# Eight-head attention layers: scores and projections as products of 32 stationary columns, one per column tile

## The reference

```python
h = group_norm(x) * gn_w + gn_b
qkv = einsum('oc,bct->bot', qkv_w, h) + qkv_b          # 8 heads of 16 channels
w = softmax(einsum('bct,bcs->bts', q * scale, k * scale))
a = einsum('bts,bcs->bct', w, v)
out = x + einsum('oc,bct->bot', proj_w, a) + proj_b
```

## Time and profile before

| | us |
|---|---|
| median of 3 runs | 2267.47 |
| the profiled execution: time | 2267.78 |
| the profiled execution: span, first to last instruction | 2265.9 |
| PE busy | 2194.3 |
| DVE busy | 1814.8 |
| ACT busy | 1719.2 |
| POOL busy | 520.5 |

### The profile page before, as it was taken

The page is one execution under the profiler, slowest core; times in us unless marked ns, Lnnn a source line. Parts: engine busy times, 40 slices in busy tenths (PEclk is TensorE's granted clock), DMA queues, the critical chain, the costliest instruction groups (busy, mean ns, idle before and its releaser), DMA issues. The chain is left out here.

```text
span 2265.9 us, 34021 instructions
## 1 busy us (share of the span) xinstructions
PE 2194.3 (97%) x11776; PEld 972.9 (43%) x11776; DVE 1814.8 (80%) x3176; ACT 1719.2 (76%) x3107; POOL 520.5 (23%) x689
## 2 busy tenths in 40 slices
PE   2999999999999999999999999999989999999998
PEld 1233232323333232333323233333327888888887
DVE  2888888888888888888888888888837777777776
ACT  1477777777877777787777777777778888888887
POOL 3113030312203030211303031130013333333331
PEclk9999999999999999999999999999999999999999
DMA  6053343516243351625334251633111112111111
GB/s 81 4 77 54 59 62 57 82 45 91 46 66 54 58 79 48 92 42 75 54 59 70 57 78 45 86 52 62 26 45 58 59 44 67 53 48 60 41 53 49
DMA packets 81646, 132.29 MB, mean 58 GB/s; under 512 B 17632, under 2 KB 50528, under 8 KB 81504
## 3 DMA queue, kind: packets, MB, share of 16 engines
q1 hardware_dynamic: 78240, 129.70, 31.9%
q10 hardware_dynamic: 3264, 0.79, 0.2%
HBM read 53.12 MB, written 17.83 MB: 31 GB/s over the span
## 5 line engine op out<-in xcount | busy, mean ns | idle before, releaser
L449 DVE TENSOR_REDUCE h_half_nmax<-h_s_ps 128x1 f32<-128x512 f32 x2048 | 1284.7, 683 | 242.5 <-PE h_s_ps L684 233.7
L600 ACT ACTIVATE h_probs<-h_st_ps 128x512 f32<-128x512 f32 x2048 | 1103.3, 599 | 359.9 <-PE h_st_ps L821 353.7
L684 PE MATMUL h_s_ps<-h_krep,h_qrep 96*128 96x512 bf16 x2048 | 794.4, 388 | 23.8 <-SPq L234 21.9
L821 PE MATMUL h_st_ps<-h_qrep,h_krep 99*128 99x512 bf16 x2048 | 778.0, 382 | 10.9 <-ACT h_probs L600 9.9
L676 PE MATMUL h_pv<-h_probs,h_vT 128*32 128x512 f32 x4096 | 546.4, 605 | 0.9 <-ACT h_probs L600 0.7
L684 PEld LDWEIGHTS h_s_ps<-h_krep,h_qrep 96*128 96x128 bf16 x2048 | 199.8, 98 | 683.4 <-DVE h_half_nmax L449 504.8
L821 PEld LDWEIGHTS h_st_ps<-h_qrep,h_krep 99*128 99x128 bf16 x2048 | 201.5, 99 | 196.5 <-issue 35.8
L1336 PE MATMUL o_s<-o_k,o_q 128*128 128x512 f32 x768 | 223.8, 427 | 8.1 <-DVE o_q L1157 5.8
L349 POOL TENSOR_SCALAR h_nparts<-h_nmax 128x16 bf16<-128x16 f32 x64 | 16.4, 256 | 927.8 <-DVE h_nmax L457 927.8
L1336 PE MATMUL o_pv<-o_pT,o_vT 128*128 128x512 f32 x768 | 207.3, 406 | 0.8 <-ACTq L1263 0.8
L1151 DVE TENSOR_TENSOR o_pT<-o_t,o_pT 128x512 fp32r<-128x512 f32 x256 | 164.5, 684 | 44.6 <-ACT o_pT L1288 42.3
(11 more groups left out here) (116 smaller groups left out, 1379.1 us busy)
## 6 DMA issues: line engine op xcount, KB each, us to landing
h_krep<-h_kp SPq DMA_DIRECT2D x96, 256.0 KB, 8.7
h_qrep<-h_qp SPq DMA_DIRECT2D x192, 128.0 KB, 6.5
x_res<-out_dram SPq DMA_DIRECT2D x24, 512.0 KB, 3.8
num<-av SPq DMA_DIRECT2D x128, 64.0 KB
rrep<-rden_dram SPq DMA_DIRECT2D x16, 512.0 KB
out_dram<-o_y SPq DMA_DIRECT2D x16, 512.0 KB
out_dram<-h_y SPq DMA_DIRECT2D x15, 512.0 KB, 2.6
o_x_in<-out_dram SPq DMA_DIRECT2D x15, 512.0 KB, 3.5
```

The costliest lines, as they stand in the source:

```text
L449: reduce = nc.vector.tensor_reduce(half_nmax[:, c, unit:unit + 1], s_ps[bank(2 * n + c)][:, :], AX.X, ALU.max, negate=True)
L600: nc.scalar.activation(probs[g % 2][:, j, :], st_ps[bank(n)][:, :], ACT.Exp, scale=1.0 / CH ** 0.5).then_inc(exp_done, 1)
L684: nc.tensor.matmul(s_ps[bank(n)][:, :], qrep[par][0:KS, th, head, tile * P:(tile + 1) * P], krep[par][0:KS, head, c * HALF:(c + 1) * HALF] ...
L821: nc.tensor.matmul(st_ps[bank(n)][:, :], krep[par][0:KM, head, st * P:(st + 1) * P], qrep[par][0:KM, th, head, :], start=True, stop=True). ...
```

## The change

The new function `in_columns` writes one product with 128 stationary columns as four, each with 32 of the columns and into 32 partitions of the same bank. The row scores, the transposed scores and all four kinds of projection go through it; only the last of the four raises the semaphore, and only the first waits. The average and the transposes are written as before.

```diff
             def project(c, column, ready):
-                nc.tensor.matmul(misc[:, :], wg[:, column:column + P], h[:, c * HALF:(c + 1) * HALF],
-                                 start=True, stop=True).then_inc(ready, 1)
+                in_columns(misc, wg[:, column:column + P], h[:, c * HALF:(c + 1) * HALF]).then_inc(ready, 1)
...
-                    product = nc.tensor.matmul(misc[:, n * P:(n + 1) * P], h[:, t * P:(t + 1) * P],
-                                               weights, start=True, stop=True)
+                    product = in_columns(misc[:, n * P:(n + 1) * P], h[:, t * P:(t + 1) * P], weights)
...
             def project_output(c):
-                nc.tensor.matmul(misc[:, :], wo[:, 0:P], attn[:, c * HALF:(c + 1) * HALF],
-                                 start=True, stop=True).then_inc(misc_for_dve, 1)
+                in_columns(misc, wo[:, 0:P], attn[:, c * HALF:(c + 1) * HALF]).then_inc(misc_for_dve, 1)
...
+            def in_columns(to, stationary, moving):
+
+                for j in range(P // 32):
+                    columns = slice(32 * j, 32 * j + 32)
+                    product = nc.tensor.matmul(to[columns, :], stationary[:, columns], moving, start=True, stop=True)
+                return product
+
             def row_scores(n, par, quad, unit, c):
...
-                nc.tensor.matmul(s_ps[bank(n)][:, :], qrep[par][0:KS, th, head, tile * P:(tile + 1) * P],
-                                 krep[par][0:KS, head, c * HALF:(c + 1) * HALF],
-                                 start=True, stop=True).then_inc(scores_ready, 1)
+                in_columns(s_ps[bank(n)], qrep[par][0:KS, th, head, tile * P:(tile + 1) * P],
+                           krep[par][0:KS, head, c * HALF:(c + 1) * HALF]).then_inc(scores_ready, 1)
...
-                            nc.tensor.matmul(st_ps[bank(n)][:, :], krep[par][0:KM, head, st * P:(st + 1) * P],
-                                             qrep[par][0:KM, th, head, :],
-                                             start=True, stop=True).then_inc(st_ready, 1)
+                            in_columns(st_ps[bank(n)], krep[par][0:KM, head, st * P:(st + 1) * P],
+                                       qrep[par][0:KM, th, head, :]).then_inc(st_ready, 1)
```

## The result

The changed kernel takes 2276.72 us (median of 10 runs, 2272.42 to 2280.63), the kernel before 2267.43 beside it (10 runs): the ratio is 1.0039, interval 1.003 to 1.0048. It is 9 us slower; 2195 was forecast, and the time lies above the range. The profiled execution took 2280.48 us with a span of 2278.5.

What follows compares the result with a forecast made beforehand. PE was taken as the bound, busy 397.7 of 400 us. Width changes save 123 us, less 3, 21, 14 and 13, leaving 72: 2267.5 - 72 = 2195 us. The range was 2165 to 2270.

Steps and rivals of the forecast that it cites:

- the width change: Around each group's value products, switching 128 to 32 columns and back costs PE 0.24 us; removing it saves 123 us.
- an exposed weight load: Rival: every score product pays 0.025 us for weights not loaded ahead; about 2250 us, chance 0.13.
- a beat of 0.06 between starts: Rival: matmuls start no faster than a fixed beat; at 0.061 us the gain is gone, near 2267, chance 0.04.
- tiles that take turns: Rival: four tiles share reads of the moving data; at half speed a score takes 0.44 us, total 3035, chance 0.09.
- The two rules of the Trainium skill: Column tiling gives up fast weight load (estimate 2257 us); about 62 ns per microcode-decoded matmul would leave no gain.
- average: Still 128 columns wide, now between 32-column neighbours, it gets a gap taken as 0.2 us, 16 images: +3 us.
- first score waits for Q copies: At the next image's first score PE waits 1.4 us for query copies that come no earlier, 15 images: +21 us.
- statistics on DVE: The next image's statistics add 0.68 us of DVE work to each of two groups, 15 images: +14 us.
- smaller DVE and ACT places: Coefficients after the average, joining half maxima, two normalising passes: 0 to 1.8 us per image, middle taken, +13 us.
- PE waits for its instructions: Rival: more loads and matmuls per group; waiting 1.4 us for each of 135 instruction packets gives 2384 us, chance 0.09.
- gaps that come every third group: Sign in the changed profile's PE groups that PE waits for instruction packets, estimated to last 3.8 groups each.
- no gap recurs today: Evidence given against PE waiting for instructions: PE's groups in the kernel before show no recurring gap.

Runs made afterwards that it cites:

- e8: Changed kernel with the projections put back to 128 columns, only the scores in four tiles; executed once more for its profile: 2218.97 us.
- e5: Changed kernel with at most two key copies under way at a time, using two semaphores in turn: 2183.27 us, ratio 0.963.
- e6: Changed kernel with at most two key copies under way, query copies released at k = 5 and sent in pairs, at most two pairs under way: 2165.6 us, ratio 0.9552.
- e7: Changed kernel with the query copies released at k = 5 in place of k = 13 and no copies paced: 2275.91 us, one execution.
- e1: Changed kernel with SP waiting for each of the six key copies before it sends the next: 2281.05 us, ratio 1.0061.

## Why the prediction was wrong

**What bounds, and the width change: right.** The gap around the value products came from changing the column width. It went away in every plain group (2.61), and e8 put one of 0.30 at the projections. 512 x 0.24 = 123 us was right.

**The rivals on the matmul itself fell.** Four tiles take 0.39 to 0.43 us where one matmul took 0.38, and the next score follows after 0.22, four matmuls and four loads: neither an exposed weight load (a step of 0.24), nor a beat of 0.06 between starts, nor tiles that take turns. (A beat of 0.061 would have cost 8 x 0.026 = 0.21 us a group, most of the 0.24 and not all of it.) The two rules of the Trainium skill weighed in the prediction (TensorEngine Tiling, Gotcha 2; TensorE: Matmul & The Clock Gate, on 62 ns per matmul) do not set the time here.

**The smaller terms: right in kind, most of them too large.** e5, which is after without the gap, can be laid beside the sum (us):

| term | forecast | measured | from |
|---|---|---|---|
| width changes | -123 | -123 | plain group 2.85 to 2.61 |
| average | +3 | +5 | its group 3.04 - 2.61, before 2.98 - 2.85: 0.30 x 16 |
| first score waits for Q copies | +21 | +18 | e5 - e6 |
| statistics on DVE | +14 | +8 | two groups of 2.87 and 2.98, before 2.90 and 2.93: 0.50 x 15 |
| smaller DVE and ACT places | +13 | +8 | the rest |
| sum | -72 | -84 | e5 against before, 2183.27 - 2267.05 |
| PE without instructions | 0 | +93 | after - e5, 2276.72 - 2183.27 |

That the two ends nearly cancel, so that the time comes out 0.4% from before, is chance.

**The step that failed** is the dismissal of "PE waits for its instructions", which put it at nothing in the sum; measured, it cost 93 us. The prediction had named the mechanism and given it 0.09, with three faults in the working. First, it took the 1.4 us that a packet needs to move as the whole of a wait, and expected a short wait at every packet, as its sign "gaps that come every third group" says. What came was one wait in each of 15 images, 3.9 us of standing still and 2.6 of half clock; the late packet came when the key copies, 13 us of them, were nearly through (835.21 of 835.7). Second, "no gap recurs today" was taken as evidence against it. But a packet can be late in before as well: none of q8 started between 896.41 and 928.55, across the key copies sent from 914.39 on. PE ran only some 350 loads and matmuls in that time, and did not run dry:

```profile
896.41:928.55 32.14, 32.14 (x180) 11.42 (x173) 25.62 (x42) 26.46 (x50) 16.03 (x11) 1.00 0.56 87
```

A packet lasted 24 us before and lasts 9 us after, and the prediction had both ends in hand: 9.4 groups to a packet now and 3.8 then (9.4 x 2.85 = 27 and 3.8 x 2.61 = 10 us; with the 254 that a packet held in e7, and not the 302 of its estimate, 7.9 and 3.2 groups). It set them against the packet's own time and never against the longest run of copies in the trace. The Q copies were named as a risk; the key copies, 1.5 MB in one go, were not looked at. Third, nothing was put down for the clock: 4 us of standing still cost 2.6 more at half clock.

The rival was to turn slower than before from 0.53 us per packet, and the 93 us are 0.69 for each of the 135. That this condition was met is partly luck, since it was meant as a wait at each packet. The range, whose upper end rested on the weight load, left the case out.

**What stays open.** Deeper queues of copies make the packets of q8 late, and e1 and e5 show that a shallower one cures it. The rows don't show when PE asks for a packet, nor in which order the requests are served. A packet need not wait for the last copy: in e8 one moved at 705.44, with key copies under way from 697.4 to 711.2, and in after a packet of the other instruction queue, q14, moved at 1132.07, between key copies. The Trainium skill (DMA: Bandwidth & Descriptors, section "Queues, rings and completion order") says that each DMA engine takes turns between its queues, packet by packet. By that a packet of q8 would have slipped in among the 837 of q1 if PE had asked for it in time; here none did between 819.7 and 834.9, so either the request came late or the rule does not hold for it, and no run here tells which.

## What to carry to other kernels

Splitting one instruction into four that run side by side cost PE no time here, but its instructions arrive by DMA in packets and must share the DMA engines with the data. Work out how long a packet lasts before and after, and compare that with the longest run of copies issued in one go, not with the time that a packet itself takes. Where the packet is the shorter, PE can run dry; whether it does depends on how many instructions it has in hand (here about two packets) and uses up in that stretch. Then limit how many copies are under way: two at once kept the copies moving and let the instructions through, one at a time was too slow.

## What the runs showed of the hardware

- With six copies of 256 KB queued no packet of q8 moved from 819.7 to 834.9; with two under way two moved in 15.4 us (e5).
- A packet of 16 KB holds 254 of PE's loads and matmuls here (e7), and PE stopped 490 to 535 after the start of the packet before the late one (after).
- A wait for instructions shows as idle time of PE "<-issue", also between two tiles of one score where the program has no wait, with DVE and ACT waiting for PE, and as a missing q8 row in that stretch.
- Standing still for 4 us was followed by 5.9 us at 0.50 of the clock.
- Six copies of 256 KB take 25.2 us one by one (e1) and 13 us in one queue (after).
- Changing from 32 to 128 columns and back costs 0.24 us around the value products and 0.30 around a projection or the average.
